# Attention in two halves of two batches, and probability transposes in two PSUM banks instead of three

## The reference

```
q = rope((x @ Wq.T).reshape(B, L, 32, 64))
k = rope((x @ Wk.T).reshape(B, L, 8, 64))
v = (x @ Wv.T).reshape(B, L, 8, 64)
p = softmax(where(causal, q @ k.T * 64**-0.5, -inf))
x = layernorm(x + (p @ v) @ Wo.T)
```

## Time and profile before

| | |
|---|---|
| median of three executions | 1506.04 us (1505.34 to 1507.19) |
| the profiled execution | 1508.23 us |
| its span, first to last instruction | 1506.4 us |
| mean granted TensorE clock | 0.946 of full speed |
| busy: PE, DVE, ACT, POOL | 1309.0, 1068.1, 907.6, 535.1 us |
| attention, first transposes to the last pass | 54.6 to 1060.0 us |

### The profile page before, as it was taken

The page is one execution under the profiler, slowest core; times in us unless marked ns, Lnnn a source line. Parts: engine busy times, 40 slices in busy tenths (PEclk is TensorE's granted clock), DMA queues, the critical chain, the costliest instruction groups (busy, mean ns, idle before and its releaser), DMA issues. The chain is left out here.

```text
span 1506.4 us, 26394 instructions
## 1 busy us (share of the span) xinstructions
PE 1309.0 (87%) x7105; PEld 1091.6 (72%) x7112; DVE 1068.1 (71%) x2572; ACT 907.6 (60%) x2137; POOL 535.1 (36%) x436
## 2 busy tenths in 40 slices
PE   3699999999999999999999999997524497899986
PEld 2588888878878887887888888886413375677775
DVE  3678878878878878887887888887756757744312
ACT  2576677667766766776676776676156373554322
POOL 3234244233433423433333433341013062544443
PEclk9799999999999999999999999999755699999998
DMA  4341122212122111222211221111334111001000
GB/s 162 113 118 42 36 53 69 55 52 56 38 58 72 44 36 49 63 54 59 56 35 43 80 51 37 50 43 29 134 115 163 42 43 42 12 32 42 1 29 28
DMA packets 47818, 88.07 MB, mean 58 GB/s; under 512 B 10960, under 2 KB 13008, under 8 KB 45648
## 3 DMA queue, kind: packets, MB, share of 16 engines
q1 hardware_dynamic: 47696, 86.82, 19.9%
HBM read 40.64 MB, written 4.19 MB: 30 GB/s over the span
## 5 line engine op out<-in xcount | busy, mean ns | idle before, releaser
L453 ACT ACTIVATE probs<-probs,neg_max 128x128 f32<-128x128 f32 (+3 forms) x512 | 285.4, 560 | 185.7 <-DVE neg_max L580 185.3
L653 DVE TENSOR_TENSOR pT_lo<-ps_t,pT_hi 128x512 fp32r<-128x512 f32 (+1 forms) x384 | 218.1, 594 | 83.5 <-ACT pT_hi L508 69.3
L724 PE MATMUL ps_s<-k_st,q_st 128*128 128x256 f32 (+2 forms) x1024 | 221.3, 338 | 27.5 <-DVE neg_max L580 25.5
L580 DVE CUSTOM_DVE_ANT_0 probs<-ps_s,mask 128x128 f32<-128x128 f32 (+3 forms) x512 | 228.2, 481 | 3.2 <-PE ps_s L724 2.6
L724 PEld LDWEIGHTS ps_s<-k_st,q_st 128*128 128x128 f32 x1024 | 158.7, 190 | 46.1 <-DVE neg_max L580 32.7
L376 POOL TENSOR_TENSOR o_lo<-o_sum,o_hi 128x512 fp32r<-128x512 f32 x64 | 82.0, 1281 | 291.4 <-ACT o_hi L468 291.4
L508 ACT ACTIVATE pT_hi<-ps_t 128x512 fp32r<-128x512 f32 (+1 forms) x384 | 174.6, 528 | 6.8 <-PE ps_t L769 3.7
L769 PE MATMUL ps_t<-ident,probs 128*128 128x128 f32 x1280 | 163.8, 276 | 14.8 <-ACT probs L453 14.8
L781 PE MATMUL ps_o<-pT_hi,v_st 128*128 128x256 f32 (+2 forms) x512 | 168.5, 340 | 0.0
L769 PEld LDWEIGHTS ps_t<-ident,probs 128*128 128x128 f32 x1280 | 143.8, 142 | 20.0 <-ACT probs L453 10.3
L781 PE MATMUL ps_o<-pT_lo,v_st 128*128 128x256 f32 (+2 forms) x512 | 155.7, 326 | 0.0
(11 more groups left out here) (195 smaller groups left out, 2940.6 us busy)
## 6 DMA issues: line engine op xcount, KB each, us to landing
q_st<-q_tmp SPq DMA_DIRECT2D x512, 64.0 KB, 2.0
k_st<-k_st SPq DMA_DIRECT2D x64, 128.0 KB, 2.3
raw<-in_wq_t SPq DMA_DIRECT2D x16, 256.0 KB, 3.1
y<-in_x_t SPq DMA_DIRECT2D x4, 1024.0 KB, 11.2
y<-in_x SPq DMA_DIRECT2D x4, 1024.0 KB, 5.9
raw<-in_wo_t SPq DMA_DIRECT2D x16, 256.0 KB, 3.0
w_gu<-in_fside_t SPq DMA_DIRECT2D x4, 1024.0 KB, 4.9
stage<-in_up_t SPq DMA_DIRECT2D x4, 1024.0 KB, 11.3
```

Source lines behind the costliest of these rows:

```text
L453: act.activation(probs[:, h % 2, SO[i]:SO[i] + SW[i]], probs[:, h % 2, SO[i]:SO[i] + SW[i]], ACT.Exp, bias=neg_max[:, h % 2, i:i + 1], sca ...
L580: dve.tensor_tensor_reduce(out=probs[:, h % 2, SO[i]:SO[i] + SW[i]], in0=ps_s[:, i % 2, 0:SW[i]], in1=mask[:, L - SW[i]:L], scale=-SCALE, ...
L653: dve.tensor_tensor(pT_lo[:, d, :], ps_t[:, k, 0:P * w].rearrange("p (w c) -> p w c", c=P), f32(pT_hi[:, d, :]), ALU.subtract).then_inc(p_ ...
L724: i = pe.matmul(dst, a, c, start=(j == 0), stop=(j == len(terms) - 1))
```

## The change

The four batches are split into two halves. All 8 groups run for batches 0 and 1 first, then all 8 for batches 2 and 3. A step is one group for one half, so there are 16 steps of two units, and every weight is loaded and split in both halves. Steps 0, 6, 7, 8, 14 and 15 are written out, 1 to 5 and 9 to 13 are two loops of the hardware. The split x holds two batches; x of batches 2 and 3 is split in step 7, two tiles in each of the passes 0 and 1 of both units, into the room of batches 0 and 1. Weights of the next step are split in batch 0 of a step. The DMAs of weights stand behind the q moves of their unit instead of ahead of them, and `load_x` of batches 2 and 3 moves from the first unit to step 7.

`ps_t` has two banks. The three groups of transposes take them in turn, `(h + k) % 2`, so group k waits until VectorE has subtracted group k − 2. The third group moves on PE behind the output projection, and its copy on ScalarE behind the first two exponentials. VectorE's order is unchanged.

```diff
+HALF = 2
+STEPS = B // HALF * HKV
-        xT_hi = sb("xT_hi", [P, B, KT, L], F32R)
-        xT_lo = sb("xT_lo", [P, B, KT, L], F32R)
+        xT_hi = sb("xT_hi", [P, HALF, KT, L], F32R)
+        xT_lo = sb("xT_lo", [P, HALF, KT, L], F32R)
-        ps_t = pb("ps_t", [P, 3, L])
+        ps_t = pb("ps_t", [P, 2, L])
-        M0_ORDER = [["odd", "vT", "kv", "even"]] * B
+        M0_ORDER = [["odd", "vT", "kv", "even"]] * HALF
         M1_ORDER = [["out3", "recip1", "out0", "out1", "recip0", "out2", "out3 early"],
-                    ["recip1", "out0", "out1", "recip0", "out2"],
-                    ["out3", "recip1", "out0", "out1", "recip0", "out2"],
-                    ["out3", "recip1", "out0", "out1", "recip0", "out2"]]
+                    ["recip1", "out0", "out1", "recip0", "out2"]]
...
         def weights_in(g, b, h):
-            last = isinstance(g, int) and g == HKV - 1
-            if b == 2 and not last:
+            if b == 0 and not is_step(g, STEPS - 1):
                 return [["kv"], ["q0", "q1"], [], []][h]
             return ["o0", "o1"] if (b, h) == (1, 0) else []
...
         def x_later(g, b, h):
-            return range(8 + 4 * h, 12 + 4 * h) if isinstance(g, int) and g == 0 and b == 0 and h < 2 else []
+            if is_step(g, HKV - 1) and h < 2:
+                return range(8 + 4 * b + 2 * h, 10 + 4 * b + 2 * h)
+            return []
-        def groups(eng, body):
-            body(0)
-            with eng.Fori(1, HKV - 1) as g:
-                body(g)
-            body(HKV - 1)
+        def steps(eng, body):
+            body(0, 0)
+            with eng.Fori(1, HKV - 2) as g:
+                body(g, 0)
+            body(HKV - 2, 0)
+            body(HKV - 1, 0)
+            body(HKV, 1)
+            with eng.Fori(HKV + 1, STEPS - 2) as g:
+                body(g, 1)
+            body(STEPS - 2, 1)
+            body(STEPS - 1, 1)
...
(SyncE)
+                    if not (last and b == HALF - 1):
+                        move_q(u + 1)
                     if b == 0:
-                        sp.wait_ge(w_lo, g * 5 + 3)
-                        load_weights(g, ["o0", "o1"])
-                    if b == 1 and not last:
-                        sp.wait_ge(w_lo, g * 5 + 5)
-                        load_weights(g + 1, ["q0", "q1", "kv"])
-                    if not (last and b == B - 1):
-                        move_q(u + 1)
+                        sp.wait_ge(w_lo, w_count(g - 1, "o1") if last else w_count(g + 1, "q1"))
+                        load_weights(g, half, ["o0", "o1"])
+                    if b == 1 and not (last or is_step(g, STEPS - 2)):
+                        sp.wait_ge(w_lo, w_count(g, "o1"))
+                        load_weights(g + 2, 1 if is_step(g, HKV - 1) or is_step(g, HKV - 2) else half, ["q0", "q1", "kv"])
...
(ScalarE, in pass h)
-                        for k in range(3):
-                            act.wait_ge(p_t, n * 3 + (k + 1))
...
+                        high_p(n, h, 0)
+                        high_p(n, h, 1)
                         for what in weights_in(g, b, h):
                             high_weights(g if what[0] == "o" else g + 1, what)
                         for t in x_later(g, b, h):
                             x_part(t)
                         if more:
                             exp(n + 1, (h + 1) % 2, 0)
                             exp(n + 1, (h + 1) % 2, 1)
+                        high_p(n, h, 2)
...
(TensorE)
-            def transpose_probs(n, h):
-                for k, blocks in enumerate(T_BANKS):
-                    wait(pe, p_lo, (n - 1) * 3 + (k + 1))
-                    pe.wait_ge(exped, n * 4 + 4)
-                    for c, (kt, qt) in enumerate(blocks):
-                        at = SO[qt] + P * kt
-                        i = pe.transpose(ps_t[:, k, P * c:P * (c + 1)], probs[:, h % 2, at:at + P], ident[:, :])
-                    i.then_inc(p_t, 1)
+            def transpose_probs(n, h, k):
+                wait(pe, p_lo, n * 3 + (k - 1))
+                pe.wait_ge(exped, n * 4 + 4)
+                for c, (kt, qt) in enumerate(T_BLOCKS[k]):
+                    at = SO[qt] + P * kt
+                    i = pe.transpose(ps_t[:, (h + k) % 2, P * c:P * (c + 1)], probs[:, h % 2, at:at + P], ident[:, :])
+                i.then_inc(p_t, 1)
...
-                        transpose_probs(n, h)
+                        transpose_probs(n, h, 0)
+                        transpose_probs(n, h, 1)
                         if more:
                             scores(*ahead, 0)
                             scores(*ahead, 1)
                         (the output projection, as before)
+                        transpose_probs(n, h, 2)
                         if more:
                             scores(*ahead, 2)
                             scores(*ahead, 3)
```

More of the change, by code:

```diff
@@ L385, in _, with body @@
                 low_k(u, u)
-            def body(g):
-                first = isinstance(g, int) and g == 0
-                last = isinstance(g, int) and g == HKV - 1
-                for b in range(B):
-                    u = g * B + b
+            def body(g, half):
+                first = is_step(g, 0)
+                last = is_step(g, STEPS - 1)
+                for b in range(HALF):
+                    u = g * HALF + b
                     for what in weights_in(g, b, 0):
@@ L404, in body @@
                     low_o(u, 0, b % 2)
-                    if not (last and b >= B - 2):
+                    if not last:
                         rotate_k(u + 2)
-            groups(pool, body)
-            low_o(HKV * B - 1, 1, 1)
+            steps(pool, body)
+            low_o(U - 1, 1, 1)
         @block.scalar
@@ L489, in _, with body @@
                 exp(0, 0, i)
-            def body(g):
-                first = isinstance(g, int) and g == 0
-                last = isinstance(g, int) and g == HKV - 1
-                for b in range(B):
-                    u = g * B + b
-                    nxt = not (last and b == B - 1)
-                    nxt2 = not (last and b >= B - 2)
+            def body(g, half):
+                first = is_step(g, 0)
+                last = is_step(g, STEPS - 1)
+                for b in range(HALF):
+                    u = g * HALF + b
+                    nxt = not (last and b == HALF - 1)
+                    nxt2 = not last
                     prev = not (first and b == 0)
```

180 lines of the change are left out of this document (93 added, 87 removed).

## The result

| | before | after |
|---|---|---|
| median | 1506.62 us (1505.34 to 1509.79, 4 runs) | 1516.94 us (1515.95 to 1517.26, 4 runs) |
| profiled execution, its span | 1508.23, 1506.4 us | 1515.95, 1514.2 us |
| granted clock, mean | 0.946 | 0.945 |

After over before is 1.0064, 95% interval 1.0047 to 1.0082: the change makes the kernel slower by 7 to 12 us. The forecast was 1509.6 (range 1501 to 1527), slower being the likeliest; it fell 7.3 us short of what was measured.

The account below looks back on a forecast made before the run. TensorE (PE) was taken to bound attention, busy 87% of the span. Terms 9.0 + 4.5 − 10.6 − 7.6 + 8.0 + 0.9 − 0.6 sum to +3.6 us, 1506.0 + 3.6 = 1509.6 us, range 1501 to 1527.

Parts of the forecast that it names:

- step 7: Four passes of step 7: splitting two x tiles in each lengthens them, +8.0 us (bounds 4 and 12).
- the tail: Last step: the early fourth projection waits for VectorE's addition to y, the next pass gets shorter; +0.9 us.
- Pairs and q weights, +13.5: Attention steps: more pairs of batches 0 and 1, +9.0 us; q weight copies lengthening head 1 of batch 0, +4.5 us.
- The loop jumps, −10.6: First pass of each loop round: shorter bodies are kept, not fetched again, so 5 × 2.1 us go, −10.6 us.
- Rival 1: At the loop's jumps back: they stay dear, 8 × 2.1 us instead of none, +20.5 us, 1526.5 us; chance 0.20.
- Two banks cost nothing: Probability transposes in every pass: two banks and the third group behind the projection cost 0; bounds −8 and +19 us.
- a transposing group waits for a subtraction: Sign of being wrong, in the profile after: PE's transposes wait for VectorE's subtraction; no size given.
- The start, −7.6: First passes: splitting x of batches 2 and 3 leaves them, and PE's wait at 115.35 shrinks; −7.6 us.
- The 2.1 us at 115.35: PE's wait early in the kernel, put down to x and weight loads queued ahead of q moves, goes: 2.1 us.
- Rivals 2 and 3: Rival 2: new order fills PE's gaps in short passes, 1501.6 us, chance 0.11; rival 3: wait every pass, +19 us, 0.07.

Follow-up runs that it names:

- The long body in after: The changed kernel with a loop body of two steps (four units), run twice per half, two jumps back in all: 1520.05 us, ratio 1.0095 to the kernel before.
- the kernel with x spread: The changed kernel with x tiles of batches 2 and 3 split over six passes of steps 6 and 7: 1505.94 us, ratio 1.0002 to the kernel before.

## Why the prediction was right, and where its sizes were off

The direction and most of the mechanism are right. The size is not: +3.6 us was forecast and 10.3 measured, just above the forecast's own range of 1504 to 1515 us. It lies inside 1501 to 1527 only because that range was drawn to take in rivals that are all out. In the traces the error is two terms that are too small, step 7 by 3.2 us and the tail by 1.0 (2.9 with the clock of the last pass), and part of both is the banks, which were put at nothing.

- *Pairs and q weights, +13.5*: right. A looped step of after measures 63.17 us on average for 62.95 + 0.3, head 1 6.85 for 6.82. The q copies alone make 0.27 us in head 1, the number that the prediction took from batches 2 and 3.
- *The loop jumps, −10.6*: right in size and place, and shown by three experiments. No jump in before: −11.6. Straight code in after: nothing but register work. The long body in after: both jumps at 10.05 to 10.45 us. Rival 1 is out. With it goes, for these bodies, the sentence of the Trainium skill, Runtime: NRT & Kernel Launch, section "Instruction fetch mechanics", that the store is a FIFO filled in sequence: no packet came in a steady round. Its other statement there, that a taken branch to code which isn't held has to fetch first, agrees with the traces of before and of the long body, where VectorE stands still for 2.65 to 3.14 us behind the jump.
- *Two banks cost nothing*: this step is the one that failed. It was worked out for a plain pass, and for a plain pass it holds (63.17 us a looped step with two banks, 63.18 with three). It left out the passes in which other work stands between ScalarE's second and third copy. There the third copy is late by all of that work, VectorE waits 1.27 us for it in head 1, and with x tiles behind it that pass is 2.4 to 3.2 us longer. Alone the banks cost 6.8 us, in the changed kernel 3.3. One of the prediction's signs of being wrong came true, that a transposing group waits for a subtraction: it does in 37 passes, 29.2 us in all, most of them short passes. The looped steps show that this costs nothing there.
- *Step 7, +8.0, measured +11.2*: the place was right, a term mis-sized. The forecast for the four passes with tiles was 10.1, 9.1, 9.1 and 8.2 us; they took 9.78, 10.92, 8.86 and 9.78. Both of the head-1 passes are 1.6 to 1.8 us over, but not for the same reason. In batch 0 it is the late third copy (the banks) and the slow subtraction. In batch 1 it is mostly the slow subtraction: VectorE waits only 0.23 us for the copy, its two x tiles take 2.52 us, and with three banks the pass is as long (9.79). The sum also left out what PE's clock loses behind a wait: the third pass took 9.51 us and not 8.24. In the two traces of the same step 7 where the clock fell once more the excess is 13.6 and 13.4 us, so the term is short by more than the 3.2 that this trace shows.
- *The start, −7.6, measured −7.3*: right for passes 0 to 2 (7.51, 6.62, 7.98 for 7.3, 6.8, 7.8). The 2.1 us at 115.35 came as said, and for the reason given: PE waited there for q moves that stood in the queue behind the x loads.
- *The tail, +0.9, measured +3.8*: the early projection was released 6.0 us into its pass, as worked out (6.5), but behind its wait the matmuls take 0.63 us in place of 0.40, and the pass took 10.39 us for 9.2. Of the rest 1.9 us do not belong to the change: the last pass ran at the lower clock in this execution, and the kernel with x spread, which is the same there, takes 18.6 us where after took 20.5. PE's rows and the granted clock (columns as above):

```profile
1036.64 0.50 PE L750 MATMUL m<-woT_hi,o_hi 128*128 128x512 f32 x1 [2.11 <-DVE y L628]
...
1037.98 0.63 PE L750 MATMUL m<-woT_lo,o_hi 128*128 128x512 f32 x1
...
1065.17 1.91 PE L795 MATMUL ps_t<-ident,probs 128*128 128x128 f32 x8
```

```profile
1022.00:1030.60 8.60, 5.88 (x39) 4.96 (x38) 6.26 (x18) 5.51 (x17) 0.98 (x1) 1.00 0.42 103
1030.60:1041.00 10.40, 8.29 (x41) 6.90 (x40) 5.57 (x16) 4.63 (x13) 1.29 (x1) 0.84 0.20 62
```

- *Rivals 2 and 3* are out. The new order does not fill PE's gap in the short passes: PE now waits 0.76 us ahead of the two transposes, for VectorE's subtraction and not for its maximum, and the pass is 7.85 us as before. The prediction had the transposes fill the gap and the last score wait instead; its price of 0 was right, its place was not. The +19 us of a wait in all passes is neither in the step nor in the median.

## What to carry to other kernels

A loop's price is read at its jump: compare the first pass of a round with the same pass elsewhere, and look at whether instruction packets move in a steady round. If they do and the first pass is longer, either shorten the body until they stop or write the loop out; both took the 2.1 us per jump away here, and writing it out made the kernel before 0.8% faster, more than anything else in this study. When a term of step 7's kind is read from one trace, look at the clock in other traces of the same code: here one pass was 8.26 or 9.87 us by that alone. When an order is judged by a plain pass, judge it again in the passes that carry extra work, with the extra instruction put where the code puts it: a copy moved behind it inherits its whole length. And before work with both inputs in SBUF is put on VectorE in "free" time, look at what GpSimd does in that time, and add what PE's clock loses if PE has to wait.

## What the runs showed of the hardware that was not expected

VectorE's subtraction of two SBUF operands (`xT_lo<-y,xT_hi`, 128x512) takes 0.68 us beside an idle GpSimd, mostly 0.8 to 1.8 us beside a busy one, and 3.62 us in the worst case; meanwhile VectorE's subtractions with one operand in PSUM (`pT_lo`) stay at 0.69. Sometimes GpSimd is the one to wait: with three banks two `wqT_lo` take it 3.79 us instead of 2.51, while VectorE's two x tiles run in 1.27. The Trainium skill, SBUF — State Buffer, section "Terms", says that VectorE and GpSimd share a pair of SBUF ports as a lock held for a whole instruction, so that the loser blocks; the traces agree. The 3.62 us fit it: three of GpSimd's instructions end 3.06 us after the subtraction starts, and it ends 0.56 us behind them.

Behind the same wait of PE, 2.3 us ahead of the seventh pass of step 7, the granted clock over the pass was 1.00 in one trace and 0.83 in four others. The pass took 8.26 us in the one and 9.76 to 9.87 in the others. What decides it was not found.

A body that reads its step from registers is slower than the same body written out: 0.3 us in the changed kernel's 63, and some 0.4 us in the four units of the kernel before, 124.6 us without the jump.
